# Attention scores on a graph: the linear weights, the square roots, the row order and the penalties moved between engines and stages

## The chip, the cores and the metric

One core of a Trainium2 chip runs the whole kernel in one launch. The metric is the device time of one execution in microseconds (us). TensorE is PE in the rows, VectorE is DVE, ScalarE is ACT, GpSimd is POOL and SyncE is SP.

## The reference

The kernel computes a graph attention layer and a mixture-of-experts layer on 2,500 nodes with 512 features; the change touches the first. Cut to what matters:

```python
x = x + gnn(layernorm(x), edge_index, W_e, W_r, a)      # 40,000 edges, sorted in the kernel by source
h_e = einsum('nf,hfd->hnd', xn, W_e)                    # 8 heads of 64
h_r = einsum('nf,hfd->hnd', xn, W_r)
a_src, a_dst, a_dif, a_abs, a_prd = split(a, 5, axis=1)
diff = h_r[:, dst] - h_r[:, src]
score = (h_e . a_src)[src] + (h_e . a_dst)[dst] + diff . a_dif + |diff| . a_abs + (h_r[src] * h_r[dst]) . a_prd
ex = exp(leaky_relu(score) - segment_max(...)[src]);  att = ex / segment_sum(ex)[src]
out = segment_sum(att * h_e[:, dst], src)
```

The terms of the score that are linear in h_e and h_r collapse to two vectors of 8 numbers a node: x times a matrix `lin` of 512 x 16 (8 columns for the source end, 8 for the other), where `lin` is W_e and W_r contracted with a_src, a_dst and a_dif.

## The kernel before, in words

`project_and_sort` is the first stage. Each engine has one list of instructions, in an order written out by hand, and semaphores between them.

- DVE sorts the 40,000 edge keys: `sort_inside(1)` to `sort_inside(9)` are n exchanges each, then `merge_near(m)` and `merge_inside()` for m = 1 to 5, then two merges (m = 6, 7) that need TensorE to turn the keys. Between them it makes the sums of the layer norm (`prepare(n, True)`), finishes the square roots (`prepare(n, False)`, for the blocks of `STAT_PARTS`: 0 to 3, 4 to 11, 12 to 19), makes `lin` (`weigh`), and finishes two blocks of table rows at a time (`finish(i)`: blocks 2i and 2i+1; it needs their squares and their linear terms `lin_sb`).
- PE counts edges into blocks (`count_blocks`, 20 small matmuls that follow ACT's `tally`), then goes through 20 blocks b: it turns block b+1 (`turn`), projects block b on W_r (`project_r`), takes its bf16 parts off (`take_mid`, `take_hi`), projects it on W_e (`project_e`) and makes the linear terms of block b-2 (`project_lin`). Five places in that order, numbered 2b (after `take_mid`) and 2b+1 (the end of block b), hold the turns of the sort keys: `KEY_TURNS`. PE waits there for `key_out`, and DVE's `come_back` waits for the turn.
- ACT makes the tallies, the square roots (`take_root(0)` among the tallies, `take_root(1)` ahead of the 20 blocks, `take_root(2)` in block 1), and for each block `normalise(b+2)`, `turned(b+1)` and the copies out of PSUM. `prepare(n, False)` on DVE waits for `take_root(n)` on ACT. `normalise(4)` and `normalise(12)` are the first that need the roots of parts 1 and 2.

`score_edges` is the second stage; it begins when every engine has ended the first. It takes 84 groups n of 512 edges. POOL gathers four tiles of rows a group (`RING` = 4 groups ahead), SP broadcasts the group's local row numbers (`spread`), DVE makes a one-hot of them, PE fetches the source rows with it (`fetch`), DVE subtracts, PE turns the difference, ACT takes |d| and a linear function of it, DVE multiplies, and PE reduces over the heads. Ahead of group 0 stand: the loads of `raw_a` and the write of `local_d` (SP, both ahead of the first `spread`), `heads`, `extra`, `cin`, `by_abs`, `by_square` (DVE, PE and ACT wait for them), and seven `penalties` (a matmul `pick` on PE and a pass on DVE each). Behind group 1 stands `lead_penalties`, one scan over 3,071 columns on DVE. `strip_scores` puts one further DVE instruction (512 columns) into each of four groups, once in 14 groups.

Of the kernel before, what the change touches and what calls it, by code (L numbers as in the profile page):

```python
# [9 lines left out]
ALU = mybir.AluOpType  # L10
# [33 lines left out]
SQUARED = frozenset(())  # L44
STAT_PARTS = (slice(0, 4), slice(4, 12), slice(12, NB))
KEY_TURNS = (29, 31, 34, 36, 38)
# [55 lines left out]
def project_and_sort(nc, k, sem, x, src, dst, we, wr, a, table_d, he_d):  # L102
# [8 lines left out]
    XB, SB, XT, AR = 6, 6, 4, 5  # L111
    with ExitStack() as ctx:
# [3 lines left out]
        a_all = s.sb("a_all", [P, HEADS, 4 * D])  # L116
        prod = s.sb("prod", [P, CH, HEADS, D])
        lin = s.sb("lin", [P, CH, 2 * HEADS])
        dif = s.sb("dif", [P, CH, HEADS])
# [34 lines left out]
        spare = prod[:, :, :, :].rearrange("p c h d -> p (c h d)")  # L154
# [10 lines left out]
        xin = [sem(f"x_in{c}") for c in range(5)]  # L165
        wrin, wein, ain = sem("w_r_in"), sem("w_e_in"), sem("a_in")
        lines_made, ident_made, number_made, window_made, made = sem("lines_made"), sem("ident_made"), sem("number_made"), sem("window_made"), sem("constants_made")
        stats, rready, rdone, normed = sem("stats"), sem("var_ready"), sem("root_done"), sem("norm_ready")
        linr, xn_ready, tp, xt_ready = sem("lin_ready"), sem("xn_ready"), sem("x_turned"), sem("xt_ready")
# [7 lines left out]
        key_out, key_turned = sem("key_out"), sem("key_turned")  # L177

        with nc.Block() as block:
            @block.sync  # L180
            def _(sp):
# [19 lines left out]
                for b in range(NB):  # L201
                    sp.wait_ge(he_ready, b + 1)
                    sp.dma_start(he_d[b * P:(b + 1) * P, :], he[:, b % 2, :]).then_inc(he_out[b % 2], 16)
                for j in range(2):
                    sp.wait_ge(he_out[j], 16 * NB // 2)

            @block.gpsimd
            def _(pool):
# [26 lines left out]
                                        fill=1.0, base=1, pattern=[[-1, P]], channel_multiplier=1))  # L235
                link(pool.memset(k["pick"][:, :, :, :, :], 0.0))
# [13 lines left out]
            def _(act):  # L250
                act.dma_start(a_all[:, :, 0:3 * D], a[:, 0:3 * D].partition_broadcast(P)).then_inc(ain, 16)
                act.dma_start(a_all[:, :, 3 * D:], a[:, 4 * D:].partition_broadcast(P)).then_inc(ain, 16)
# [56 lines left out]

                for t in range(8):  # L310
                    tally(t)
# [28 lines left out]
            def _(pe):  # L340
# [58 lines left out]

                pe.wait_ge(window_made, 1)  # L400
# [17 lines left out]
                project_lin(NB - 2)  # L418
                project_lin(NB - 1)
                pe.wait_ge(key_out, 6)  # L420
# [3 lines left out]
            def _(dve):  # L424
# [22 lines left out]
                def weigh():  # L447

                    dve.wait_ge(ain, 32)
                    dve.wait_ge(wrin, 16 * CH)  # L450
                    dve.wait_ge(wein, 16 * CH)
                    w4e = w_e[:, :, :].rearrange("p c (h d) -> p c h d", h=HEADS)
                    w4r = w_r[:, :, :].rearrange("p c (h d) -> p c h d", h=HEADS)
                    for w, piece, out in ((w4r, 2, dif[:, :, :]), (w4e, 0, lin[:, :, 0:HEADS]), (w4e, 1, lin[:, :, HEADS:])):
                        link(dve.tensor_tensor(prod[:, :, :, :], w, bcast(a_all[:, :, piece * D:(piece + 1) * D], 1, CH), ALU.mult))
                        link(dve.tensor_reduce(out, prod[:, :, :, :], AX_X, ALU.add))
                    mark(dve.tensor_tensor(lin[:, :, 0:HEADS], lin[:, :, 0:HEADS], dif[:, :, :], ALU.subtract))
                    dve.tensor_tensor(lin[:, :, HEADS:], lin[:, :, HEADS:], dif[:, :, :], ALU.add).then_inc(linr, 1)
                    link(dve.tensor_scalar(a_all[:, :, 3 * D:], a_all[:, :, 3 * D:], 0.5, None, ALU.mult))

                def finish(i):
# [4 lines left out]
                    link(dve.tensor_tensor(both, both, bcast(a_all[:, :, 3 * D:], 1, 2), ALU.mult))  # L466
# [98 lines left out]
                weigh()  # L565
# [3 lines left out]
                prepare(2, True)  # L569
                sort_inside(7)  # L570
                prepare(2, False)
                sort_inside(8)
                finish(0)
                sort_inside(9)
                insert_pads()
                for m in range(1, 6):
                    merge_near(m)
                    merge_inside()
                    finish(m)
                for m in (6, 7):  # L580
# [6 lines left out]
                    if m == 6:  # L587
                        finish(6)

                dve.nop().then_inc(key_out, 1)  # L590
                finish(7)
# [15 lines left out]
                link(dve.scalar_tensor_tensor(k["local_rows"][:, :], is_pad, float(P), part, ALU.mult, ALU.add))  # L607
                link(dve.tensor_scalar(part, whole, 12, None, ALU.logical_shift_right))
# [3 lines left out]
                finish(8)  # L612
                finish(9)
# [9 lines left out]
def score_edges(nc, k, sem, a, table_d, local_d):  # L623
# [6 lines left out]
    RING = 4  # L630
    hrs, lins, att = k["hrs"], k["lins"], k["att"]
    with ExitStack() as ctx:
# [5 lines left out]
        raw = s.sb("raw_a", [P, 2, CH])  # L638
# [3 lines left out]
        heads = s.sb("heads", [P, 62])  # L642
        by_abs = s.sb("by_abs", [P, CH, 62])
        by_square = s.sb("by_square", [P, CH, 62])
# [11 lines left out]
        cin = s.sb("cin", [1, 2, CH, 16, 2])  # L656
# [6 lines left out]
        ain, wready = sem("score_a_in"), sem("score_weights")  # L663
        picked, penned = sem("runs_picked"), sem("penalties")
        got = [sem(f"rows_in{j}") for j in range(RING)]
        local_out, locs = sem("locals_out"), [sem(f"locals_in{j}") for j in range(RING)]
# [8 lines left out]
        multiplied = lambda n: CH * sum(i not in SQUARED for i in range(n + 1))  # L675

        with nc.Block() as block:  # L677
            @block.sync
            def _(sp):
                for half in range(2):  # L680
                    for n, piece in enumerate((3, 4)):
                        sp.dma_start(raw[half * D:(half + 1) * D, n, :],
                                     a.rearrange("(c t) f -> f c t", t=2)[piece * D:(piece + 1) * D, :, half],
                                     allow_slow_non_contiguous=True).then_inc(ain, 16)
                sp.dma_start(local_d[:, :], k["local_rows"][0:G, :]).then_inc(local_out, 16)
                sp.wait_ge(local_out, 16)
# [21 lines left out]
            def _(dve):  # L708
                link = k["dve_chain"].on(dve)
                mark = k["dve_chain"].mark  # L710
                mark(dve.memset(heads[:, :], 0.0))
                mark(dve.memset(extra[:, :, :, :, :, :], 0.0))
                link(dve.memset(cin[:, :, :, :, :], 0.0))
                mark(dve.memset(heads[0:D, 30:31], 1.0))
                mark(dve.memset(heads[D:P, 31:32], 1.0))
                dve.wait_ge(ain, 64)
                link(dve.tensor_scalar(raw[:, 1, :], raw[:, 1, :], -0.5, None, ALU.mult))
# [958 lines left out]
```

## Time and profile before

| | us |
|---|---|
| median of 3 runs | 1646.72 (1646.37 to 1648.43) |
| the profiled execution | 1648.01 |
| its span, first to last instruction | 1646.3 |
| first stage | 0 to 234.4 |
| second stage, first group's first subtraction | 247.74 |

The span is 1.7 us shorter than the execution that it was taken from, and that execution 1.3 us longer than the median. Times in rows are from the start of the span.

### The profile page before, as it was taken

What the parts mean: (1) busy time and instruction counts of PE and PEld (TensorE: products, weight loads), DVE (VectorE), ACT (ScalarE), POOL (GpSimd) and SP (SyncE); (2) the same over time, 40 slices, a digit from 0 to 9 for tenths busy, and PEclk for the clock granted to TensorE, in tenths of its full rate; (3) what the DMA queues carried; (4) which work ended last, traced back from release to release, by engine and by line L of the source; (5) the groups of instructions that cost most, each with busy time, mean ns of one, the idle gap of its engine ahead of it and who ended that gap; (6) DMA issues with size and microseconds to landing.
All of it is one profiled execution on the core that took longest, in us unless ns stands there. A gap on an engine that the chain in (4) does not pass through costs nothing. (4 is left out here: it accounts for less than half of the span.)

```text
span 1646.3 us, 25232 instructions
## 1 busy us (share of the span) xinstructions
PE 1305.9 (79%) x6421; PEld 745.9 (45%) x6422; DVE 1212.5 (74%) x2399; ACT 980.8 (60%) x2411; POOL 884.1 (54%) x982
## 2 busy tenths in 40 slices
PE   5799948999999999995688888888880702999950
PEld 1355524555555555552344444444440301777730
DVE  8898578999999999997588888888889320222216
ACT  3455516998989898984677777777770300333310
POOL 2000036666666666662677777777767055555520
PEclk9899968999999999997799999999995955999985
DMA  6111136777777777760877766676660821333329
GB/s 209 39 58 53 58 113 172 213 205 199 208 198 207 199 207 199 208 184 2 288 194 209 200 198 201 200 201 199 199 187 2 306 103 33 115 127 127 128 96 348
DMA packets 114111, 271.34 MB, mean 165 GB/s; under 512 B 27650, under 2 KB 43766, under 8 KB 113738
## 3 DMA queue, kind: packets, MB, share of 16 engines
q0 software_dynamic: 64160, 207.60, 43.4%
q1 hardware_dynamic: 47754, 61.26, 11.1%
q10 hardware_dynamic: 2080, 1.05, 0.2%
q8 instruction: 58, 0.95, 0.2%
q14 instruction: 59, 0.48, 0.1%
HBM read 236.42 MB, written 33.43 MB: 164 GB/s over the span
## 5 line engine op out<-in xcount | busy, mean ns | idle before, releaser
L1096 PE MATMUL m_ps<-msg,hot 128*128 128x512 f32 x672 | 368.4, 638 | 73.8 <-ACT msg L1038 64.6
L701 POOL DMA_INDIRECT x_sb<-table_d,target x336 | 333.0, 991 | 174.6 <-PE d_ps L871 86.8
L1015 POOL DMA_INDIRECT g<-he_d,target x336 | 339.6, 1011 | 132.9 <-issue 78.7
L945 ACT ACTIVATE uv<-ab,raw_a 128x512 f32<-128x512 f32 x336 | 274.3, 816 | 11.3
L858 PE MATMUL gs_ps<-room,hot_t 128*128 x1008 | 276.4, 384 | 1.7 <-DVE hot_t L724 1.7
L1059 DVE TENSOR_TENSOR msg<-g,room 128x384 f32<-128x384 f32 x336 | 185.7, 553 | 84.9 <-DMA g<-he_d,target 81.4
L731 DVE TENSOR_TENSOR x_sb<-x_sb,gs_ps 128x512 f32<-128x512 f32 x336 | 229.2, 682 | 17.8 <-PE lin_ps L862 11.5
L940 ACT ACTIVATE ab<-d_ps 128x512 f32<-128x512 f32 x336 | 196.1, 584 | 73.4 <-PE d_ps L871 71.5
L1038 ACT ACTIVATE msg<-g,room 128x64 f32<-128x64 f32 x672 | 170.2, 339 | 111.9 <-DMA g<-he_d,target 111.7
L735 DVE TENSOR_TENSOR uv<-uv,ab 128x512 f32<-128x512 f32 x336 | 230.2, 685 | 3.3 <-ACT uv L945 2.8
L1066 DVE TENSOR_TENSOR room<-m_ps,room 128x512 f32 x336 | 229.8, 684 | 0.6
L871 PE MATMUL d_ps<-ident,x_sb 128*128 128x128 f32 x1344 | 213.9, 282 | 6.9 <-DVE x_sb L731 6.1
L1098 PEld LDWEIGHTS den_ps<-room,hot 128*128 128x128 f32 x672 | 128.7, 191 | 162.6 <-issue 162.6
L871 PEld LDWEIGHTS d_ps<-ident,x_sb 128*128 128x128 f32 x1344 | 141.8, 141 | 51.4 <-DVE x_sb L731 12.8
L858 PEld LDWEIGHTS gs_ps<-room,hot_t 128*128 128x128 bf16 x1008 | 92.6, 98 | 111.7 <-issue 69.8
L1096 PEld LDWEIGHTS m_ps<-msg,hot 128*128 128x128 f32 x672 | 102.5, 193 | 78.7 <-issue 77.9
L1532 DVE TENSOR_TENSOR hid_in<-h_ps,b_sb 128x256 f32<-128x256 f32 x47 | 20.0, 425 | 145.1 <-PE h_ps L1468 145.1
L245 POOL DMA_DIRECT2D table_d<-row x20 | 11.1, 562 | 204.9 <-DVE row L471 204.9
L1030 ACT ACTIVATE off<-iota,local 128x128 f32<-128x128 f32 x336 | 107.0, 395 | 0.3 <-PEq L677 0.3
L891 PE MATMUL sc_ps<-uv,heads 128*32 128x512 f32 x672 | 91.2, 615 | 12.0 <-DVE uv L735 12.0
L1098 PE MATMUL den_ps<-room,hot 128*128 128x8 f32 x672 | 96.0, 215 | 0.0
L1468 PE MATMUL h_ps<-w_sb,xt 128*128 x376 | 90.6, 385 | 0.0
(284 smaller groups left out, 1711.7 us busy)
## 6 DMA issues: line engine op xcount, KB each, us to landing
x_sb<-local_d SPq DMA_DIRECT2D x84, 128.0 KB
w_sb<-in_L_ffn_W_dram SPq DMA_DIRECT2D x16, 512.0 KB, 9.2
pair_rows<-pairs_d SPq DMA_DIRECT2D x8, 1024.0 KB, 13.0
x_sb<-table_d,target POOLq DMA_INDIRECT x336
g<-he_d,target POOLq DMA_INDIRECT x336
table_d<-row POOLq DMA_DIRECT2D x20, 260.0 KB, 2.6
he_d<-he SPq DMA_DIRECT2D x20, 256.0 KB, 2.0
xn_d<-xn SPq DMA_DIRECT2D x10, 512.0 KB, 4.0
```

The lines of the kernel that those rows point to most:

```text
L701: pool.indirect_dma_start(gd[:, r, t, :], None, table_d, bass.IndirectOffsetOnAxis(ap=k["target"][:, q + t:q + t + 1], axis=0)).then_inc(g ...
L731: dve.tensor_tensor(row, row, gs_ps[:, (GT * n + t) % 3, :], ALU.subtract).then_inc(dready, 1)
L735: dve.tensor_tensor(uv[:, n % 2, c, :], uv[:, n % 2, c, :], ab[:, n % 2, c, :], ALU.mult).then_inc(vr, 1)
L858: pe.matmul(gs_ps[:, (GT * n + t) % 3, :], h, hrs[:, bass.ds(blk, 1), piece, :].rearrange("p a f -> p (a f)"), start=(piece == 0), stop=(p ...
L871: last = pe.transpose(d_ps[:, c % 2, t * P:(t + 1) * P], gd[:, n % RING, t, c * P:(c + 1) * P], k["ident"][:, :])
L940: act.activation(ab[:, j, c, :], d_ps[:, c % 2, :], ACT.Abs).then_inc(abr, 1)
L945: act.activation(uv[:, j, c, :], ab[:, j, c, :], ACT.Identity, bias=raw[:, 0, c:c + 1], scale=raw[:, 1, c:c + 1]).then_inc(ur, 1)
L1015: pool.indirect_dma_start(g[:, r, t, :, :, :].rearrange("p c h d -> p (c h d)"), None, he_d, bass.IndirectOffsetOnAxis(ap=k["target"][:, q ...
L1059: dve.tensor_tensor(msg[:, r, t, 0:HV, :, :], g[:, r, t, 0:HV, :, :], bcast(weight, 3, D), ALU.mult).then_inc(made, 1)
L1066: dve.tensor_tensor(to, m_ps[:, i % BK, :], to, ALU.add).then_inc(added, 1)
L1096: pe.matmul(m_ps[:, i % BK, :], hot[:, r, t, :], msg[:, r, t, :, :, :].rearrange("p c h d -> p (c h d)"), start=True, stop=True).then_inc( ...
L1098: pe.matmul(den_ps[:, bass.ds(blocks[t] * HEADS, HEADS)], hot[:, r, t, :], att[:, tg * GT + t, :, strip, :], start=False, stop=True, skip_ ...
```

## The change

- `lin` is made on PE: ACT's DMA queue loads three pieces of `a` turned (`a_rows`, six loads of single elements), POOL lays them on diagonals (`a_cols`), PE turns W_r and W_e in eight steps of four transposes (`turn_weights`: four ahead of `turn(0)`, four behind the last count), ACT copies each out (`keep_turned_weights`), and PE multiplies: 32 matmuls with 16 columns (`weigh`), ahead of block 0. DVE's `weigh` goes.
- `take_root(1)` moves from ahead of the blocks to block 1, `take_root(2)` from block 1 to block 7. On DVE, `prepare(2, False)` moves behind `sort_inside(8)`.
- `finish(0)` comes ahead of `sort_inside(8)`, `finish(1)` behind `prepare(2, False)`, and each later one a merge sooner; `finish(9)` ahead of the last `key_out`. `KEY_TURNS` are later.
- `raw_a` is loaded by ACT's queue at the kernel's start (four loads of single elements, ahead of ACT's first instruction), and `heads`, `cin` and its scaling are POOL's, in the first stage. `local_d` is written by SP at the end of the first stage.
- In the second stage the seven penalties go to groups 2 to 8 (`PICK_AT` = 2), and the scan becomes six of 512 columns in groups 9 to 14 (`LEAD_AT` = 9). The unused branch `SQUARED` goes, with `by_abs` and `by_square`.

```diff
-KEY_TURNS = (29, 31, 34, 36, 38)
+KEY_TURNS = (33, 34, 38, 40, 41)
...
-    XB, SB, XT, AR = 6, 6, 4, 5
+    XB, SB, XT, AR = 6, 6, 4, 4
...
+                sp.wait_ge(key_out, 6)
+                sp.dma_start(local_d[:, :], k["local_rows"][0:G, :]).then_inc(local_out, 16)
...
@@ scalar
-                act.dma_start(a_all[:, :, 0:3 * D], a[:, 0:3 * D].partition_broadcast(P)).then_inc(ain, 16)
-                act.dma_start(a_all[:, :, 3 * D:], a[:, 4 * D:].partition_broadcast(P)).then_inc(ain, 16)
+                for half in range(2):
+                    for piece in range(3):
+                        act.dma_start(a_rows[half * D:(half + 1) * D, piece, :],
+                                      a.rearrange("(c t) f -> f c t", t=2)[piece * D:(piece + 1) * D, :, half],
+                                      allow_slow_non_contiguous=True).then_inc(arin, 16)
+                act.dma_start(a_prd[:, :, :], a[:, 4 * D:].partition_broadcast(P)).then_inc(ain, 16)
+                for half in range(2):
+                    for n, piece in enumerate((3, 4)):
+                        act.dma_start(k["raw_a"][half * D:(half + 1) * D, n, :],
+                                      a.rearrange("(c t) f -> f c t", t=2)[piece * D:(piece + 1) * D, :, half],
+                                      allow_slow_non_contiguous=True).then_inc(rawin, 16)
...
+                for i in range(4):
+                    keep_turned_weights(i)
                 turned(0)
                 for t in range(14, NB):
                     tally(t)
-                take_root(1)
+                for i in range(4, 8):
+                    keep_turned_weights(i)
+                act.wait_ge(lin_summed, 1)
+                act.copy(lin[:, :, :], l_ps[:, 0:CH * 2 * HEADS].rearrange("p (c x) -> p c x", c=CH)).then_inc(linr, 1)
                 for b in range(NB):
                     if b == 1:
+                        take_root(1)
+                    if b == 7:
                         take_root(2)
...
@@ tensor
+                def weigh():
+                    pe.wait_ge(cols_ready, 1)
+                    pe.wait_ge(w_kept, 2 * CH)
+                    for c in range(CH):
+                        for i in range(2 * CH):
+                            last = pe.matmul(l_ps[:, c * 2 * HEADS:(c + 1) * 2 * HEADS], w_t[:, i // CH, i % CH, c * P:(c + 1) * P],
+                                             a_cols[:, 1 - i // CH, i % CH, :], start=(i == 0), stop=(i == 2 * CH - 1))
+                    last.then_inc(lin_summed, 1)
...
                 pe.wait_ge(ident_made, 2)
+                for i in range(4):
+                    turn_weights(i)
                 turn(0)
                 count_blocks(14, NB)
+                for i in range(4, 8):
+                    turn_weights(i)
+                weigh()
...
@@ vector
-                weigh()
                 prepare(1, True)
                 sort_inside(6)
                 prepare(1, False)
                 prepare(2, True)
+                dve.wait_ge(ain, 16)
+                link(dve.tensor_scalar(a_prd[:, :, :], a_prd[:, :, :], 0.5, None, ALU.mult))
                 sort_inside(7)
+                finish(0)
+                sort_inside(8)
                 prepare(2, False)
-                sort_inside(8)
-                finish(0)
+                finish(1)
                 sort_inside(9)
...
@@ score_edges, tensor
                 for n in range(G + 2):
                     if n < G:
                         blocks = blocks_of(n)
+                    if 0 <= n - PICK_AT <= TG:
+                        pick(n - PICK_AT)
```

## Rows read from the trace of the kernel before

**Rows 1.** The timeline of DVE: start, length, line, tiles.

```profile
25.93 2.29 DVE L455 TENSOR_TENSOR prod<-w_r,a_all 128x2048 f32<-128x2048 f32 x1
...
40.53 4.85 DVE L436 BATCH_NORM_STATS2 st<-x_sb 128x6 f32<-128x512 f32 x8
...
63.31 0.20 DVE L94 RECIPROCAL rstd<-root 128x8 f32<-128x8 f32 x1
...
64.48 0.42 DVE L483 TENSOR_TENSOR key<-key 128x256 f32<-128x256 f32 x1
...
70.84 1.23 DVE L466 TENSOR_TENSOR sq<-sq,a_all 128x1024 f32<-128x1024 f32 x1
...
78.58 0.18 DVE L470 TENSOR_TENSOR lin_src<-lin_sb,own 128x16 f32<-128x16 f32 x1 [5.26 <-ACT lin_sb L308]
...
229.52 0.32 DVE L620 TENSOR_TENSOR lins<-lin_rest,lins 128x160 bf16<-128x160 f32 x1
```

**Rows 2.** Groups of DVE, 0 to 300 us: busy, mean, idle before, releaser.

```profile
L517 DVE COPY key<-k_ps 128x512 f32<-128x512 f32 x4 | 2.8, 692 | 16.2 <-PE k_ps L397 16.2
...
L470 DVE TENSOR_TENSOR lin_src<-lin_sb,own 128x16 f32<-128x16 f32 x10 | 1.8, 175 | 9.7 <-ACT lin_sb L308 9.5
```

**Rows 3.** The timeline of PE in the first stage.

```profile
50.45 4.97 PE L356 MATMUL r_ps<-w_r,xt 128*128 128x512 f32 x8
...
69.54 0.64 PE L346 MATMUL t_ps<-ident,xn 128*128 128x128 f32 x4
...
77.31 0.96 PE L373 MATMUL l_ps<-lin,xt 128*128 128x16 f32 x8
78.12 0.64 PE L346 MATMUL t_ps<-ident,xn 128*128 128x128 f32 x4
```

**Rows 4.** The timeline of ACT at the start.

```profile
1.93 1.28 ACT L254 ACT_TABLE_LOAD   x1 [1.93 <-issue]
...
7.96 4.94 ACT L261 ACTIVATE above<-src_i,block_edge 80x500 bf16<-80x500 int32 x8 [4.54 <-DMA dst_i<-in_dst_dram]
```

**Rows 5.** The timelines of POOL and SP where the stages meet.

```profile
228.56 1.07 POOL L245 DMA_DIRECT2D table_d<-row  x2 [1.73 <-DVE row L471]
...
244.03 0.94 POOL L701 DMA_INDIRECT x_sb<-table_d,target  x1 [0.30 <-issue]
...
234.39 2.69 SPq L682 DMA_DIRECT2D raw_a<-in_L_gnn_a_dram  x4
...
240.69 45.38 SPq L690 DMA_DIRECT2D x_sb<-local_d  x11
```

**Rows 6.** PE's timeline, then PE and clock by stretch (columns in the header).

```profile
1278.27 4.34 PE L1265 MATMUL t_ps<-ident,xn 128*128 128x128 f32 x20 [39.76 <-DVE xn L1292]
...
core 0: us, PE busy (x) PEld busy (x) DVE busy (x) ACT busy (x) POOL busy (x), PEclk, DMA share, GB/s
...
1282.00:1286.00 4.00, 3.87 (x13) 1.01 (x12) 2.60 (x6) 1.13 (x2) 0.00 (x0) 1.00 1.02 378
...
216.45:220.45 4.00, 2.89 (x25) 2.73 (x24) 3.72 (x10) 1.99 (x5) 0.13 (x1) 1.00 0.52 199
220.45:222.00 1.55, 0.43 (x3) 0.32 (x2) 1.40 (x3) 0.17 (x1) 0.00 (x0) 0.50 0.00 0
```

**Rows 7.** DVE's timeline: first subtractions of groups 1 and 5.

```profile
252.47 0.68 DVE L731 TENSOR_TENSOR x_sb<-x_sb,gs_ps 128x512 f32<-128x512 f32 x1
...
283.57 0.68 DVE L731 TENSOR_TENSOR x_sb<-x_sb,gs_ps 128x512 f32<-128x512 f32 x1
```

**Rows 8.** DVE's timeline, one row a group: groups 17 to 20.

```profile
357.50 0.25 DVE L741 TENSOR_REDUCE lin_sum<-lin_ps 128x32 f32<-128x96 f32 x1
...
363.19 0.25 DVE L741 TENSOR_REDUCE lin_sum<-lin_ps 128x32 f32<-128x96 f32 x1
...
369.45 0.25 DVE L741 TENSOR_REDUCE lin_sum<-lin_ps 128x32 f32<-128x96 f32 x1
...
376.29 0.24 DVE L741 TENSOR_REDUCE lin_sum<-lin_ps 128x32 f32<-128x96 f32 x1
```

More of the change, by code:

```diff
@@ L163, in project_and_sort @@
         k_ps = s.ps("k_ps", [P, F])
-        xin = [sem(f"x_in{c}") for c in range(5)]
+        xin, arin = [sem(f"x_in{c}") for c in range(5)], sem("a_rows_in")
         wrin, wein, ain = sem("w_r_in"), sem("w_e_in"), sem("a_in")
@@ L235, in _ @@
                                         fill=1.0, base=1, pattern=[[-1, P]], channel_multiplier=1))
+                link(pool.memset(a_cols[:, :, :, :], 0.0))
+                pool.wait_ge(arin, 16 * 6)
+                diagonal = lambda w, half, first: a_cols[half * D:(half + 1) * D, w, :, :].rearrange("p c x -> p (c x)")[:, first + half::2 * HEADS + 2]
+                for half in range(2):
+                    part = slice(half * D, (half + 1) * D)
+                    link(pool.tensor_copy(diagonal(0, half, 0), a_rows[part, 0, :]))
+                    link(pool.tensor_copy(diagonal(0, half, HEADS), a_rows[part, 1, :]))
+                    link(pool.tensor_scalar(diagonal(1, half, 0), a_rows[part, 2, :], -1.0, None, ALU.mult))
+                    link(pool.tensor_copy(diagonal(1, half, HEADS), a_rows[part, 2, :]))
+                pool.nop().then_inc(cols_ready, 1)
+                link(pool.memset(k["heads"][:, :], 0.0))
+                link(pool.memset(k["heads"][0:D, 30:31], 1.0))
+                link(pool.memset(k["heads"][D:P, 31:32], 1.0))
+                link(pool.memset(k["cin"][:, :, :, :, :], 0.0))
+                pool.wait_ge(rawin, 64)
+                link(pool.tensor_scalar(k["raw_a"][:, 1, :], k["raw_a"][:, 1, :], -0.5, None, ALU.mult))
                 link(pool.memset(k["pick"][:, :, :, :, :], 0.0))
@@ L578, in _ @@
                     merge_inside()
-                    finish(m)
+                    finish(m + 1)
                 for m in (6, 7):
@@ L630, in score_edges @@
     RING = 4
+    PICK_AT, LEAD_AT = 2, 2 + TG + 1
     hrs, lins, att = k["hrs"], k["lins"], k["att"]
+    raw, heads, cin = k["raw_a"], k["heads"], k["cin"]
     with ExitStack() as ctx:
@@ L661, in score_edges @@
         lin_row = lin_ps[:, 0, :]
-        ain, wready = sem("score_a_in"), sem("score_weights")
-        picked, penned = sem("runs_picked"), sem("penalties")
+        picked = sem("runs_picked")
         got = [sem(f"rows_in{j}") for j in range(RING)]
-        local_out, locs = sem("locals_out"), [sem(f"locals_in{j}") for j in range(RING)]
+        locs = [sem(f"locals_in{j}") for j in range(RING)]
         lin_summed = sem("lin_summed")
@@ L674, in score_edges @@
         order = [(tg, st) for tg in range(TG) for st in range(STRIPS)]
-        multiplied = lambda n: CH * sum(i not in SQUARED for i in range(n + 1))
+        use = lambda n, t: GT * n + t + min(max(n - PICK_AT + 1, 0), TG + 1)
         with nc.Block() as block:
@@ L679, in _ @@
             def _(sp):
[L680 to L686, printed above, removed]
                 for n, (tg, st) in enumerate(order):
@@ L774, in strip_scores @@
                         link(dve.tensor_reduce(fpart[:, tg:tg + 1], first, AX_X, ALU.max))
-                penalties()
+                link(dve.memset(extra[:, :, :, :, :, :], 0.0))
                 one_hot(0)
-                multiplies = lambda n: 0 <= n < G and n not in SQUARED
+                inside = lambda n: 0 <= n < G
                 for n in range(G + 2):
+                    if 0 <= n - PICK_AT <= TG:
+                        penalties(n - PICK_AT)
                     if n < G:
                         subtract(n, 0)
-                    if multiplies(n - 2):
+                    if inside(n - 2):
                         times(n - 2, 3)
@@ L879, in reduce @@
                     column = slice(30 - 2 * st, 62 - 2 * st)
[L880 to L892 removed]
+                    pe.wait_ge(vr, CH * n + CH)
+                    for c in range(CH):
+                        last = pe.matmul(sc_ps[32 * c:32 * (c + 1), :], heads[:, column], uv[:, n % 2, c, :],
+                                         start=(st == 0), stop=False, tile_position=(0, 32 * c), skip_group_check=True)
                     last.then_inc(red, 1)
@@ L1629, in kernel_body @@
                     runs=e.sb("runs", [P, F], BF16),
+                    raw_a=e.sb("raw_a", [P, 2, CH]), heads=e.sb("heads", [P, 62]),
+                    cin=e.sb("cin", [1, 2, CH, 16, 2]),
                 )
-                project_and_sort(nc, k, sem, x, src, dst, we, wr, a, table_d, he_d)
+                project_and_sort(nc, k, sem, x, src, dst, we, wr, a, table_d, he_d, local_d)
                 score_edges(nc, k, sem, a, table_d, local_d)
```

152 lines of the change are left out of this document (65 added, 87 removed).

## Prediction

> **What bounds the kernel now.** The page first (PE 79% of the span, DVE 74%), but an average over stages decides nothing; then the timelines of DVE, PE and ACT over the first stage. DVE has work from 8 us to its last instruction there, which ends at 229.84 [rows 1], and sat idle only where it asked PE or ACT for something: 16.2 us for the turned keys and 9.7 us for linear terms [rows 2]. PE goes through the blocks at one per 8.58 us (69.54 to 78.12) with no gap [rows 3]. So the first stage has two long streams side by side, hand-tied at a few places, and what matters is which of them waits at each tie. Then the timelines where the stages meet: table rows leave at 228.56, the second stage starts at 234.4 [rows 5], and its first subtraction comes 13.3 us later. In its groups PE is full, and a group takes 5.69 us (357.50 to 363.19) [rows 8].
>
> **DVE's weigh.** Removed: 25.93 to 40.53, 14.6 us of DVE [rows 1]. That is worth 14.6 us only if nothing that DVE waits for stays where it is.
>
> **When PE begins block 0 (T0).** ACT now issues eleven loads ahead of its first instruction. SP issued four such loads of single elements in 2.69 us, 0.67 each [rows 5]; ten of them, 0.6 for the broadcast and the start at 0.8 give 8.1; table load and first root 1.5 [rows 4]; first tally at 9.7 instead of 7.96. (It also frees DVE and ACT from the long broadcast ahead of `dst`, worth nothing, since ACT is the later one.) A tally takes 0.62 (4.94 for 8) [rows 4]: fourteen and a root 8.7, so 18.4, and PE's count ends 0.6 behind, at 19.0. Four steps of transposes follow. At the low clock level 20 transposes took 4.34 us [rows 6], so a step is 0.87: 22.5; `turn(0)` 23.4; ACT's copy 24.1; six tallies 27.8, PE's last count 28.4; four more steps 31.9, and the last copy 32.6. `AR` 5 to 4 costs nothing: PE follows each tally within one. The POOL work for `a_cols` (eight small instructions from about 9) and the weights' loads are in by then (DVE read both weights from 25.93 on without a wait [rows 1]).
>
> Then PE's `weigh`: 32 fp32 matmuls, two instructions each, 64, of just the form of `project_lin`, of which 8 take 0.81 us (77.31 to 78.12) [rows 3]. At the full level 6.5 us; at the low one twice that, 13. Here the level is the open price. PE is low when this begins. Twenty transposes back to back brought it up: 0.50 before (PE had idled 39.8 us), 1.00 from 1282 on [rows 6]. On the other side, a stretch of mostly `project_lin` matmuls, 2.89 of 4.00 us busy, ended with the level down to 0.50 at 220.45 [rows 6]; back to back they may do better. Between 6.5 and 13 I take 8.4: a low start, then the full level. T0 = 32.6 + 8.4 = 41.0; bounds 39.1 and 45.6, and in the latter case block 0 starts low too: its first projection took 4.97 in place of about 3.6 us [rows 3], so 47.2.
>
> The Trainium skill ("TensorE: Matmul & The Clock Gate", Part 4: PE-mode transpose) says that transposes do not count as work for the clock. By that rule PE's `weigh` would be low throughout and the sum that of rival A; the trace disagrees, with its 20 transposes.
>
> **The square roots: the wait that takes weigh's place.** `take_root(1)` now stands on ACT behind all of block 0, which follows T0: about T0 + 8.7 = 49.7. DVE arrives for it at 36 (25.93 and 5.6 for the sums and 4.8 for six exchanges). It waits some 13 us: weigh's whole saving. Next `finish(0)` asks for block 1's linear terms (block 3 of PE, T0 + 32.8): 9 us, in place of 5.26 before [rows 1]. Then the long one: `take_root(2)` stands behind ACT's `keep_mid(6)`. PE's blocks 0 and 1 take 7.8 (no linear part), blocks 2 to 5 8.58 each, and block 6 up to `take_hi` 7.8, with copy and root 1.3: T0 + 58.9 = 99.9. DVE, with `sort_inside(8)` done, is there at about 80 and waits 20 us. Queued behind it are `finish(1)`, the rest of the sort, and all else of the stage.
>
> From there DVE has: its stream from 63.31 to 229.84 of before, 166.5, less its waits 25.9 [rows 2], less `sort_inside(8)` (64.48 to 70.84, 6.4) and `finish(0)` (70.84 to 78.58 less 5.26, and 0.3: 2.8), now done earlier [rows 1]: 131.5. Its ties to PE, at the new `KEY_TURNS`: the first, second and fourth turns find PE already waiting (0.7 each for the turn itself, and PE stands still for them); place 38 is reached at T0 + 168.6, DVE is there at T0 + 162.6: 6.0. So DVE ends at T0 + 58.9 + 131.5 + 8.1 = T0 + 198.5 = 239.5, against 229.84. The moved `finish` calls are the same ten and cost nothing by place (rows 2 ahead of the ring's reuse: block 10 needs `finish(2)`'s rows out at about T0 + 90, which they are). PE has spare time at the end, so its 11 to 20 us of new work cost only through T0.
>
> **The meeting of the stages.** Before, the last rows (issued 228.56 + 1.07, landing 2.6 later as the page has it) were out near 231.7, and the stage began 2.7 later [rows 5]. After: `local_d` leaves at the last `key_out`, 2.2 ahead of DVE's end, and its write takes 3.6 (237.1 to 240.69) [rows 5]: DVE's end + 1.4, + 2.7. Second stage at 239.5 + 4.1 = 243.6, before 234.4: **+9.2**.
>
> **Its prologue.** Gone: 2.69 of `raw_a` issues, the write, the memsets and penalties ahead of group 0. Next late are the gathers: group 1's last was issued at 244.03, 9.6 into the stage [rows 5], and lands about 3 later, so group 1's first subtraction comes at 13.2 into it, not 18.1 (252.47) [rows 7]: **-4.9**. PE has group 0's tiles fetched by then; the clock is low in both.
>
> **Scan and penalties.** Before, groups 1 to 5 took 31.1 us (252.47 to 283.57) [rows 7] where four at 5.69 are 22.8: the scan, and PE's fall to the low level behind it, cost 8.3. After: one more DVE instruction of 512 columns in a group made it 6.26 (0.57 more), the two later ones 0.48; one with a scan 6.84 (1.15) [rows 8]. Six penalties at 0.5, a short one at 0.15, six scans at about 1.07 (the form before ran a little shorter per column) and the ends 0.2: 9.8. PE's `pick`, a fifth of a microsecond, is under DVE's. **+1.5**; from -8.3 (all hidden) to +2.2. The heads', cin's and raw_a's work on POOL is free: POOL idles there until `finish(0)`. `SQUARED` was empty: nothing.
>
> **Sum.** +9.2 - 4.9 + 1.5 = +5.8. On the profiled execution (1648.01, span 1646.3) 1653.8; on the median 1646.72, which is what is forecast, **1652.5**. A measurement tells about 0.2%, 3.3 us, from no change.
>
> **Rivals.**
> A, PE's `weigh` wholly at the low level: T0 acts as 47.2, +6.2: 1658.7. For it: `project_lin` did not hold the level at 220; against it: the transposes ahead. By the skill's rule this is the case.
> B, ACT's loads back up, SP's own had to queue in the first 20 us, and the first tally comes 3 us later: 1655.5. For it: 2,560 single elements; against: SP's four went at an even 0.67.
> C, faster: the second stage's pieces hide in DVE's free time. Place: groups 2 to 14; price: the 9.8 in the loop falls to about 0, so 5.8 - 9.8 = -4.0: 1642.7. It decides only once they cost under 0.7 together. DVE has 0.2 free per group, against it stand the 0.48 to 1.15 of [rows 8].
> D, the waits move but cost little: T0 at its floor (every step of PE at the full level, 36.5 to 37.5), and the loop at +0: -4 and -1.5 against the forecast, no change: 1647. For it: PE worked on and off since 9 us.
>
> **How the numbers follow.** Forecast 0.48, with its own range 1649.5 to 1655.5 (T0 39 to 43, loop +0 to +2.2); A 0.25; B 0.07; C 0.08; D 0.12. Range 1645.5 to 1660: it leaves out C and a tail of A and B. Faster by over 0.2%: C and a little of D, 0.10. Within 0.2% (to 1650.0): most of D and the forecast's low end, 0.17. Slower: 0.73.
>
> **What would show it.** In the trace after: T0 (the second `turn`, block 1's) near 41, with `weigh`'s 64 matmuls at 0.1 or 0.2 each; DVE idle for `root` twice, about 13 and 20 us, the second ending near 100; DVE's last instruction near 239.5; first subtraction of group 1 13.2 into the second stage; groups 3 to 8 at 6.2 and 10 to 14 at 6.8. It is wrong if ACT reaches block 7 before 85, if the root waits are short, or if groups 2 to 14 keep 5.7.

## The result, and the profile after

The changed kernel ran at a median of 1660.63 us (1658.14 to 1662.18, four runs) beside 1646.55 of the kernel before: 1.0082 times its time (1.0064 to 1.0099), 14 us more. The sign was forecast, the size was not: +5.8 had been worked out, and +14.1 lies just above the range. The profiled execution, read below, is the fastest of the four (1658.14, span 1656.4, 10.1 longer than before's span).

ACT's timeline after: start, length, line.

```profile
0.80 4.91 ACTq L274 DMA_DIRECT2D a_rows<-in_L_gnn_a_dram  x6
5.75 0.77 ACTq L277 DMA_DIRECT2D a_prd<-in_L_gnn_a_dram  x1
6.54 4.58 ACTq L280 DMA_DIRECT2D raw_a<-in_L_gnn_a_dram  x4
11.16 1.28 ACT L284 ACT_TABLE_LOAD   x1 [11.16 <-issue]
...
12.56 3.71 ACT L291 ACTIVATE above<-src_i,block_edge 80x500 bf16<-80x500 int32 x6
...
59.24 0.22 ACT L295 ACTIVATE root<-var 128x8 f32<-128x8 f32 x1
...
109.64 0.22 ACT L295 ACTIVATE root<-var 128x8 f32<-128x8 f32 x1
```

The first six loads of single elements take 0.82 each and the last four 1.15, not 0.67, so the first tally starts at 12.56, 2.9 later than forecast (7.96 before [rows 4]). Both roots stand nearly 10 us later than forecast (59.24 for 49.7, 109.64 for 99.9).

PE's timeline after, and the granted clock of that stretch (second fence: us, PE busy, PEld busy, DVE, ACT, POOL, PEclk, DMA share, GB/s).

```profile
30.75 1.97 PE L448 MATMUL r_ps<-ident,w_e 128*128 128x128 f32 x8
32.51 1.91 PE L448 MATMUL e_ps<-ident,w_e 128*128 128x128 f32 x8
35.19 13.81 PE L457 MATMUL l_ps<-a_cols,w_turned 128*128 128x16 f32 x64 [0.77 <-ACT w_turned L342]
48.84 1.09 PE L387 MATMUL t_ps<-ident,xn 128*128 128x128 f32 x4
49.72 5.09 PE L397 MATMUL r_ps<-w_r,xt 128*128 128x512 f32 x8
...
74.58 0.64 PE L387 MATMUL t_ps<-ident,xn 128*128 128x128 f32 x4
```

```profile
35.20:37.00 1.80, 1.80 (x9) 1.80 (x9) 1.33 (x4) 0.00 (x0) 0.00 (x0) 0.50 0.00 0
37.00:49.00 12.00, 12.00 (x58) 12.00 (x58) 0.00 (x0) 0.00 (x0) 0.00 (x0) 0.50 0.01 1
```

PE's `weigh` stays at the 1.2 GHz level (0.50) from end to end, though PE is never idle in it: 13.81 us for 64. T0 is 48.84. PEld is as busy as PE: each of the 64 has 128 columns of weights to load for 16 of work. The last row is block 4's turn, from where PE goes on at 8.58 a block: it is 5.0 later than before (69.54 [rows 3]).

DVE's waits in the first stage (us in total, times, longest), and its last instruction there.

```profile
DVE rstd L93 <- ACT root L295: 46.3, 3, 23.0
DVE key L571 <- PE k_ps L438: 8.8, 4, 6.0
DVE lin_src L524 <- ACT lin_sb L338: 8.8, 1, 8.8
```

```profile
250.05 0.33 DVE L675 TENSOR_TENSOR lins<-lin_rest,lins 128x160 bf16<-128x160 f32 x1
```

The waits for turned keys and linear terms, 25.9 us before [rows 2], are 17.6; in their place, and in that of the 14.6 us of DVE's `weigh` [rows 1], stand 46.3 us for roots. DVE ends at 250.38, 20.5 later than before.

Where the stages meet, on SP; then on DVE the first subtraction of group 1, and `lin_sum` of groups 7, 8, 10, 11, 14 and 18.

```profile
248.15 0.33 SPq L207 DMA_DIRECT2D local_d<-local_rows  x1
252.92 1.74 SPq L734 DMA_DIRECT2D x_sb<-local_d  x4
```

```profile
267.23 1.28 DVE L764 TENSOR_TENSOR x_sb<-x_sb,gs_ps 128x512 f32<-128x512 f32 x2 [2.66 <-DMA x_sb<-table_d,target]
...
307.75 0.24 DVE L774 TENSOR_REDUCE lin_sum<-lin_ps 128x32 f32<-128x96 f32 x1
...
313.42 0.24 DVE L774 TENSOR_REDUCE lin_sum<-lin_ps 128x32 f32<-128x96 f32 x1
...
325.73 0.24 DVE L774 TENSOR_REDUCE lin_sum<-lin_ps 128x32 f32<-128x96 f32 x1
...
332.56 0.24 DVE L774 TENSOR_REDUCE lin_sum<-lin_ps 128x32 f32<-128x96 f32 x1
...
353.09 0.24 DVE L774 TENSOR_REDUCE lin_sum<-lin_ps 128x32 f32<-128x96 f32 x1
...
377.52 0.25 DVE L774 TENSOR_REDUCE lin_sum<-lin_ps 128x32 f32<-128x96 f32 x1
```

The second stage starts at 252.9 (18.5 later [rows 5]); a group with a scan takes 6.83. At group 18 the kernel is 14.3 behind (377.52 against 363.19 [rows 8]), and 14.2 at the last group. Behind that, in stages that the change leaves as they were, this execution made up 4.5 us (PE's first turn of the expert layer at 1287.99 against 1278.27 [rows 6]). So the 14.3 of this trace and the 14.1 of the medians agree better than the two profiled spans do, which is in part chance.

### The profile page after: what moved, and what is told of

Same layout as the page of the kernel before. It is cut to its first block and busy times, and to the rows that moved or that the text cites. A ratio compares the mean times of both kernels' runs of the same rounds, so it can differ in the third digit from the quotient of the medians.

```text
span 1656.4 us, 25442 instructions
## 1 busy us (share of the span) xinstructions
PE 1324.8 (80%) x6517; PEld 766.4 (46%) x6518; DVE 1196.3 (72%) x2389; ACT 984.5 (59%) x2420; POOL 885.1 (53%) x996
## 5 line engine op out<-in xcount | busy, mean ns | idle before, releaser
L764 DVE TENSOR_TENSOR x_sb<-x_sb,gs_ps 128x512 f32<-128x512 f32 x336 | 228.1, 680 | 17.9 <-DMA x_sb<-table_d,target 7.7
```

Source lines behind the costliest of these rows:

```text
L764: dve.tensor_tensor(row, row, gs_ps[:, use(n, t) % 3, :], ALU.subtract).then_inc(dready, 1)
```

## The experiments

The twelve runs (ten kernels, two of them run twice) came in three sets, each beside the kernel before. In the second set (1804.3 behind the difference) before took 1804.3 us. The first stage took no longer there (DVE's end at 212.35 and 212.05 for one kernel in two sets), so across sets both the ratios and the differences in us are to be looked at. "Block 4's turn" is when PE starts it, "from there" the time to the end of DVE's last instruction in the first stage, "DVE's end".

| kernel | weigh on | block 4's turn | from there | DVE's end | ratio to before (95%) | us against before |
|---|---|---|---|---|---|---|
| before | DVE | 69.54 | 160.3 | 229.84 | 1 | 0 |
| after | PE | 74.58 | 175.8 | 250.38 | 1.0082 (1.0064 to 1.0099) | +14.1 |
| x1_roots | PE | 74.30 | 174.0 | 248.31 | 1.0072 (1.0058 to 1.0085) | +12.6 |
| x2_roots_keys | PE | 72.81 | 165.9 | 238.72 | 1.0026 (1.0015 to 1.0036) | +3.3 |
| x3_raw_sp | PE | 65.44 | 175.4 | 240.86 | 1.0054 (1.0041 to 1.0068) | +8.2 |
| x4_second_stage | DVE | 69.37 | 160.3 | 229.64 | 0.9986 (0.9977 to 0.9995) | -2.6 |
| x5_first_stage | PE | 70.84 | 175.6 | 246.41 | 1.0097 (1.0077 to 1.0116) | +19.4 (1804.3) |
| x6_swapped | PE | 66.51 | 175.6 | 242.08 | 1.0040 (1.0028 to 1.0053) | +8.9 (1804.3) |
| x7_order | DVE | 52.71 | 159.6 | 212.35 | 0.9908 (0.9888 to 0.9928) | -15.2 (1804.3) |
| x8_order_second | DVE | 52.90 | 159.7 | 212.55 | 0.9853 (0.9830 to 0.9876) | -25.2 (1804.3) |
| y1_pe_repaired | PE | 61.73 | 154.7 | 216.41 | 0.9893 (0.9878 to 0.9909) | -17.0 |
| y2_weigh_later | DVE | 72.56 | 160.3 | 232.87 | 1.0013 (1.0004 to 1.0022) | +3.0 |
| y3_both_again | DVE | 53.32 | 157.9 | 211.19 | 0.9863 (0.9848 to 0.9878) | -21.6 |
| y4_order_again | DVE | 52.76 | 159.3 | 212.05 | 0.9887 (0.9872 to 0.9902) | -16.5 |

### The roots alone: x1_roots

```diff
                 for i in range(4, 8):
                     keep_turned_weights(i)
+                take_root(1)
                 act.wait_ge(lin_summed, 1)
...
-                    if b == 1:
-                        take_root(1)
-                    if b == 7:
+                    if b == 1:
                         take_root(2)
```

> The kernel after, with only two instructions of ACT moved: take_root(1) ahead of the wait for PE's weigh, take_root(2) into block 1; nothing is left out. The forecast's theory (the root waits set DVE's end): the trace of after has DVE idle 46.3 us for roots, 23.0 in the longest wait; with them gone DVE ends 15 to 20 us sooner, and the kernel runs 15 us below after. Stream theory (PE's pass over the 20 blocks, which starts at T0 and stands still only for key turns placed late, sets when DVE can end; a root wait only moves the idle time forward): the waits come back as waits for turned keys, DVE's end moves from 250.4 to about 249, the kernel runs 1 us below after.

The same order of PE with 46 us less of root waits: DVE's end moved by 2.1, the median by 1.9, to 1658.76. DVE's waits in the first stage:

```profile
DVE lin_src L523 <- ACT lin_sb L338: 28.3, 5, 17.1
DVE key L570 <- PE k_ps L437: 15.7, 4, 8.0
...
DVE sq L519 <- ACT room L319: 13.6, 1, 13.6
...
DVE rstd L93 <- ACT root L295: 3.1, 1, 3.1
```

The 46.3 us for roots are 3.1, and the other waits rose from 17.6 to 57.6: the idle time moved behind the work that used to follow it. The forecast had priced the root waits as the place where the time is lost; they were where it shows. The stream theory holds in both of its times (249 and 1 us); that the waits would come back as waits for turned keys was half of it, since most came back as waits for linear terms (28.3) and for ACT's step ahead of them in `finish` (13.6).

### The roots and the key turns: x2_roots_keys

```diff
-KEY_TURNS = (33, 34, 38, 40, 41)
+KEY_TURNS = (31, 33, 36, 37, 39)
```

> As the run with both roots early, and KEY_TURNS (31, 33, 36, 37, 39) in place of (33, 34, 38, 40, 41); nothing is left out. The forecast's theory: the places of the turns cost only their 6 us wait of the fourth one, so at most 6 us below the run with the roots alone. Stream theory: with DVE early the places are what holds it; DVE ends near 240.5, 9 us below the run with the roots alone and 10 below after. Neither reaches the kernel before: T0 itself is 20 us later than in before.

DVE's end 238.72, 9.6 below the roots alone, and the median 9.2 lower (1649.52). Of the 9.6, 1.5 came ahead of block 4, where PE's `weigh` took 11.82 in place of 13.81 (its first 2 us at the full level), and 8.1 behind it. The places of the turns in PE's order are the next tie. They can probably be this early only because DVE is there in time; the turns without the roots were not run.

### The loads: x3_raw_sp

```diff
@@ sync
+                for half in range(2):
+                    for n, piece in enumerate((3, 4)):
+                        sp.dma_start(k["raw_a"][half * D:(half + 1) * D, n, :], ...).then_inc(rawin, 16)
@@ scalar
-                for half in range(2):
-                    for n, piece in enumerate((3, 4)):
-                        act.dma_start(k["raw_a"][half * D:(half + 1) * D, n, :], ...).then_inc(rawin, 16)
```

> The kernel after, with raw_a's four loads of single elements on SP behind the loads of x in place of ACT's first list; nothing is left out. Theory of the loads (in after they took 6.54 to 11.12 on ACT, ahead of its first table load, and everything behind them follows: tallies, T0, PE's blocks, DVE's end): first tally at about 8, T0 and DVE's end 4.5 us sooner, kernel 4.5 us below after. Rival (T0 is not what sets the first stage's end, or PE waits for the weights or a_cols instead): the first tally is 4.5 sooner and the kernel within 1.5 us of after.

ACT's and PE's timelines, and the granted clock:

```profile
7.42 4.91 ACT L291 ACTIVATE above<-src_i,block_edge 80x500 bf16<-80x500 int32 x8
...
100.49 0.22 ACT L295 ACTIVATE root<-var 128x8 f32<-128x8 f32 x1
```

```profile
29.54 10.94 PE L457 MATMUL l_ps<-a_cols,w_turned 128*128 128x16 f32 x64 [0.77 <-ACT w_turned L342]
40.32 1.09 PE L387 MATMUL t_ps<-ident,xn 128*128 128x128 f32 x4
```

```profile
28.00:28.50 0.50, 0.50 (x4) 0.37 (x2) 0.47 (x8) 0.50 (x1) 0.00 (x0) 0.50 1.03 385
31.50:32.50 1.00, 1.00 (x11) 1.00 (x10) 0.97 (x4) 0.00 (x0) 0.00 (x0) 1.00 0.11 17
33.50:40.40 6.90, 6.90 (x34) 6.90 (x35) 0.03 (x1) 0.00 (x0) 5.30 (x8) 0.50 0.00 0
```

The first tally came 5.1 us sooner, T0 8.5 (weigh itself was 2.9 shorter, its first 3 us at the full level), the second root 9.2, DVE's end 9.5, the median 6.3. At the last group of the second stage the 9.2 are still there (754.35 for 763.59); behind it some of this is lost again, and no run says to what. T0, root and end move as one; from block 4's turn on it is 175.4 us, as in after (175.8). By chance this kernel is a test of the forecast's arithmetic: it has the T0 that was forecast (40.32 for 41.0), and the second root at 100.5 for 99.9 and DVE's end at 240.9 for 239.5 follow. Up to the end of the first stage, what was wrong was T0, for the most part.

### PE's weigh turned round: x6_swapped

```diff
-                    for c in range(CH):
-                        for i in range(2 * CH):
-                            last = pe.matmul(l_ps[:, c * 2 * HEADS:(c + 1) * 2 * HEADS], w_t[:, i // CH, i % CH, c * P:(c + 1) * P],
-                                             a_cols[:, 1 - i // CH, i % CH, :], start=(i == 0), stop=(i == 2 * CH - 1))
+                    for i in range(2 * CH):
+                        last = pe.matmul(l_ps[0:2 * HEADS, :], a_cols[:, 1 - i // CH, i % CH, :], w_t[:, i // CH, i % CH, :],
+                                         start=(i == 0), stop=(i == 2 * CH - 1))
+                    ... (ACT copies the 16 x 512 out, four transposes bring it back)
```

> The kernel after with PE's weigh turned round: a_cols is the stationary side and 8 matmuls of 512 columns go over the turned weights, then ACT copies 16 x 512 and 4 transposes bring it back; nothing is left out. It asks for the clock level of this stretch. In after the 64 instructions of 16 columns took 13.81 us, low throughout. Block 0's projection in after (8 instructions of 512 columns) took 5.09 with a low start against 3.60 at the full level, so the long ones raise the level within a few us. Theory (the narrow matmuls keep the level down): 16 instructions of 512 columns take about 9 us, 2 more for the copy and transposes, T0 near 46 and the kernel 2 to 4 below after. Rival (the level is down because of what PE did before, whatever comes now): 14.4 us and 2, T0 near 52, the kernel 2 to 3 above after.

PE's timeline, and the granted clock:

```profile
34.61 7.03 PE L460 MATMUL l_ps<-w_turned,a_cols 128*16 128x512 f32 x16 [0.77 <-ACT w_turned L344]
42.30 0.42 PE L465 MATMUL l_ps<-ident,he 16*128 16x16 f32 x4 [0.67 <-ACT he L361]
```

```profile
34.60:41.60 7.00, 6.99 (x16) 1.46 (x16) 1.59 (x5) 0.00 (x0) 0.00 (x0) 1.00 0.00 0
```

Sixteen instructions of 512 columns ran at 2.4 GHz, 7.03 us in place of 13.81; the next turn came at 42.65, 6.2 sooner than in after, and DVE's end at 242.08, 8.3 sooner (block 0 starts at the full level as well); from block 4's turn on it is again 175.6. Both theories had priced this too high: I had expected 9 us or 14. The comparison with after is not quite a fair one, since here the level had risen just ahead (the last eight transposes took 1.65 in place of 1.91). The next kernel is fairer: there the narrow ones begin at the full level too.

### The halves apart: x4_second_stage and x5_first_stage

The first is `project_and_sort` of before and `score_edges` of after; the second is the reverse.

> The kernel before with only the second stage's part of the change: raw_a loaded in the first stage (by SP, behind x), heads, cin and raw_a's scaling on POOL, local_d written at the end of the first stage, penalties in groups 2 to 8, the scan in groups 9 to 14; nothing is left out. By what the trace of after showed (prologue 4.4 shorter, loop +0.2, end to stage start 2.5 against 4.6): 4 to 6 us below before. By the forecast's terms (-4.9, +1.5, 0.5 at the meeting): 4 us below. Rival (the write of local_d was hidden behind the table rows, and low-clock stretches of PE eat the rest): within 1.5 us of before.

> The kernel after with the second stage of before (raw_a loaded again there, local_d written there, penalties ahead of group 0, the scan behind group 1); nothing of the reference is left out. If the two halves of the change add up (the second stage's part alone gave 2.6 us): 2 to 4 us above after, about 17 above before, all of it in the first stage, which ends near 250.4 on DVE. By the forecast's terms the first stage would be worth 9.2: 1655.5. Rival (the first stage of after costs less than its 20 us because something else is hidden there): under 12 above before.

The second stage's part alone is worth 0.14% (2.6 us at the median, 0.8 to 3.8 by its interval; the two profiled spans differ by 5.1), between both expectations and too near them to choose. The first stage's part alone is 0.97%, or 19.4 us (13.9 to 20.9 by its interval). With the second's it gives 0.83% for the whole, where 0.82% was measured, or 16.8 us, where 14.1 were: they add up within these intervals. By the forecast's terms the first stage should have cost 0.6%, 9 to 10 us, and under 12 was the rival's. The expectation missed one thing: DVE's end was 246.41 and not near 250.4, since in this execution the level was up ahead of `weigh` and for its first microsecond, and T0 came at 45.69.

In x5_first_stage the clock was at the full level when weigh began:

```profile
30.43 1.09 PE L445 MATMUL r_ps<-ident,w_e 128*128 128x128 f32 x8
31.36 1.04 PE L445 MATMUL e_ps<-ident,w_e 128*128 128x128 f32 x8
33.32 12.53 PE L454 MATMUL l_ps<-a_cols,w_turned 128*128 128x16 f32 x64 [0.93 <-ACT w_turned L339]
```

```profile
33.30:34.30 1.00, 0.98 (x9) 1.00 (x10) 0.97 (x3) 0.00 (x0) 0.00 (x0) 1.00 0.00 0
34.30:35.30 1.00, 1.00 (x9) 1.00 (x8) 0.97 (x4) 0.00 (x0) 0.00 (x0) 0.71 0.00 0
35.30:45.70 10.40, 10.40 (x51) 10.40 (x50) 2.52 (x7) 0.00 (x0) 0.00 (x0) 0.50 0.01 2
```

The transposes still ran at it (eight in 1.09, in place of 1.97), it fell within 2 us of the start of the narrow matmuls, and it stayed down for the other ten, PE busy throughout. In x3_raw_sp the level was up for their first 3 us and then fell, with nothing but such matmuls on PE since 29.54, back to back. So it is the shape, and no idle time, that costs some 6 us here. Which side of the shape, the 16 columns or the weight load that each of the 64 has, no run separates. At the full level x3_raw_sp did 11 of the narrow ones in a microsecond, so 64 would be about 6 us (an estimate from that row): turning them round saves no work on PE, it keeps the level.

### Another order, weigh on DVE: x7_order and y4_order_again

Before had lost its time to order too: PE stood 14.1 us in block 0, whose end waits on ACT for a buffer, and ACT stood behind `take_root(1)`, which needs sums that DVE makes behind its own `weigh`. PE's timeline and ACT's, before:

```profile
49.20 0.61 PE L378 MATMUL r_ps<-room,minus_bf 128*128 128x512 bf16 x1 [14.05 <-ACT room L289]
```

```profile
46.30 0.21 ACT L265 ACTIVATE root<-var 128x8 f32<-128x8 f32 x1 [20.86 <-DVE var L441]
```


```diff
-KEY_TURNS = (29, 31, 34, 36, 38)
+KEY_TURNS = (29, 30, 33, 34, 36)
...
-                    if b == 1:
+                    if b == 5:
                         take_root(2)
...
                 sort_inside(5)
-                weigh()
                 prepare(1, True)
                 sort_inside(6)
                 prepare(1, False)
-                prepare(2, True)
+                weigh()
                 sort_inside(7)
-                prepare(2, False)
+                prepare(2, True)
                 sort_inside(8)
                 finish(0)
                 sort_inside(9)
+                prepare(2, False)
```

> The kernel before with only its order changed: DVE's weigh moved behind prepare(1, False), take_root(2) to block 5, prepare(2, True) behind sort_inside(7), prepare(2, False) behind sort_inside(9), KEY_TURNS (29, 30, 33, 34, 36); nothing is left out. It asks whether the goal of the change (DVE's 25.9 us of idle time in the first stage) can be had with weigh on DVE. Stream theory: block 1 starts when lin and the first roots are there, the PE stream is then early enough for every key turn, DVE ends near 210 in place of 229.8 and the kernel runs 20 us below before. Rival (ring of rows, writes of h_e or the copies on ACT hold PE, the same 25.9 us of waits appear elsewhere): DVE's end within 5 us of 229.8 and the kernel within 5 us of before.

> The new order of the first stage alone, once more beside the other runs of this set; nothing is left out. As measured before: DVE's end 17.5 us below before's, ratio 0.989 to 0.991, 15 to 18 us below before.

DVE's end 212.35 and 212.05 (210 expected), ratios 0.9908 and 0.9887, that is 15.2 and 16.5 us below before where 20 had been expected. DVE's waits in the first stage, y4_order_again:

```profile
DVE key L517 <- PE k_ps L397: 6.2, 4, 2.3
...
DVE lin_src L470 <- ACT lin_sb L308: 1.7, 2, 1.1
```

The 25.9 us [rows 2] are 7.9, with all of `weigh`'s 14.6 us still on DVE. PE's block 4 starts at 52.8 in place of 69.54, and the time from there is that of before (159.3).

### Weigh's place alone: y2_weigh_later

```diff
                 sort_inside(5)
-                weigh()
                 prepare(1, True)
                 sort_inside(6)
                 prepare(1, False)
+                weigh()
```

> The kernel before with one edit: DVE's weigh behind prepare(1, False); nothing is left out. Stream theory: PE no longer stands 14 us for room in block 0 (which follows the roots of part 1), but 18 us for lin in block 2, and the key turns stay at (29, 31, 34, 36, 38): DVE ends at 231, the kernel within 3 us of before. Rival (what the whole new order won, all came from weigh's place): 15 us or more below before.

DVE's end 232.87, +3.0 us. PE's stall moved one block on and grew (17.9 us in place of 14.1): block 4 starts 3.0 later, and DVE's end is 3.0 later. The size is the expected one, the reason isn't: I had PE waiting for `lin` in block 2, but it waits at the end of block 1, again for ACT, which stands behind `take_root(2)`:

```profile
57.94 0.21 ACT L265 ACTIVATE root<-var 128x8 f32<-128x8 f32 x1 [21.67 <-DVE var L441]
```

So the second root had to move with it. What the root, the places of `prepare(2, ...)` and the key turns are worth one by one in this order was not run.

### Both: x8_order_second, y3_both_again; and PE's version repaired: y1_pe_repaired

The first two are one kernel, x7_order's edit with x4_second_stage's. The third is after with x1, x3 and x6, the row order of before, and `KEY_TURNS = (27, 29, 32, 34, 36)`.

> The kernel with the new order of the first stage and the second stage's part of the change together; nothing is left out. If they add up: 22 to 23 us below before (20 and the 2.6 measured for the second part alone). Rival (both live off the same idle time at the meeting of the stages): no further gain over the new order alone.

> The kernel with the new order of the first stage and the second stage's part of the change once more, beside the other runs of this set; nothing is left out. As measured before: ratio to before 0.985 to 0.988, that is 20 to 25 us.

> The kernel after with all that its traces showed late taken back, and weigh still on PE: operands swapped (that stretch took 7.03 us at the full level), raw_a's loads on SP, both roots early, finish and prepare(2, False) in the order of before, KEY_TURNS (27, 29, 32, 34, 36); nothing is left out. Stream theory: T0 near 37, no wait for a late tie, DVE ends at 217 to 221 in place of 229.8, and with the second stage's 2.6 the kernel runs 10 to 14 us below before. Rival (with weigh on PE the first blocks are too late for any order of the rest): DVE ends at 230 or later and the kernel is not below before by more than 3 us.

The new order with the second stage's part runs at 1625.61 (1624.22 to 1626.78), 21.6 below before and 35 below after; in the second set it is 25.2 below before. Over the order alone the second part is worth 5.2 in this set and 10.0 in the second, and alone it was 2.6. So it doesn't vanish beside the order, as the rival had it, but its size is not settled. PE's version repaired runs at 1630.20, DVE's end 216.41 (217 to 221 expected), T0 37.86, 3 us better than the hoped-for 10 to 14. So weigh may stand on PE, and it beats before there. It stays 5 us behind the order with `weigh` on DVE at DVE's end: from block 4 on it is 3.2 shorter without weigh on DVE, but block 4 starts 8.4 later, behind PE's eight steps and its sum.

## Why the prediction was right in sign and wrong in size

By its own steps, with what each should have been; they add up to 14.3.

| step | forecast | measured |
|---|---|---|
| first tally | 9.7 | 12.56 |
| PE's `weigh` | 8.4 | 13.65 to the next turn |
| T0 | 41.0 | 48.84 |
| second root | T0 + 58.9 | T0 + 60.8 |
| from there to DVE's end | 139.6 | 140.7 |
| DVE's end | 239.5 | 250.38 |
| to the second stage | +4.1 | +2.5 |
| second stage starts later by | 9.2 | 18.5 |
| prologue, to group 1's first subtraction | -4.9 | -3.8 |
| scan and penalties, from there to group 18 | +1.5 | -0.4 |
| sum | +5.8 | +14.3 (+14.1 at the median) |

**The step that failed is T0**, by 7.8 us, where +14.3 is 8.5 above +5.8, in two terms (the steps between them took 0.3 less than forecast). The larger, 5.3, is the level of PE's `weigh`: 8.4 was taken between 6.5 and 13 because 20 transposes had once raised the clock [rows 6]. The row on the other side, the fall during `project_lin`'s matmuls [rows 6], was the nearer one: the same form of instruction, and x3_raw_sp and x5_first_stage show it happen from the full level. Rival A had this with its price (+6.2) and was given 0.25. On the rule of the Trainium skill ("TensorE: Matmul & The Clock Gate", Part 4: PE-mode transpose) that transposes do not count as work for the clock: it led to the right time by way of a reason that these runs don't bear out. In x5_first_stage it was the matmuls of 16 columns that lost the full level, behind transposes that had it, and in x3_raw_sp the level rose from 0.50 behind sixteen transposes (25.10 to 28.78), to 1.00 as `weigh` began. The smaller term, 2.9, is the price of a load of single elements: 0.67 was taken from SP's four at 234.4; ACT's cost 0.82 and 1.15, and the same four on SP in x3_raw_sp, at 21.7 us, 1.38 (5.52 in all). So it isn't a matter of ACT's queue alone; what sets it was not tried. That was rival B (+3, 0.07). The two rivals don't exclude one another, and the forecast had no case in which both came true: +6.2, +3 and +5.8 make +15.0, or 1661.7. Each was held against the forecast singly, and the range ended at 1660, below their sum.

The second root's 1.9 beyond T0 is block 0 on a low start (9.46 to the next turn in place of 7.8), which rival A had in its 47.2.

**Right:** that weigh's 14.6 us on DVE would not be gained since both roots hang on PE's blocks; from T0 to DVE's end the chain was right within 3 us (201.5 for 198.5), with waits of 23.0 and 19.7 for 13 and 20 (7.8 of the first one's excess is T0). "Rows 2 ahead of the ring's reuse" was not quite so: ACT waited 2.4 us once for a table row to leave, with no trace of it at DVE's end. A group with a scan took 6.83 for 6.84, a group with a penalty 6.11 for 6.2. The smaller terms were off by 1 to 2 us and made up for one another: the meeting by 1.6 and the scan and penalties by 1.9 too high, the prologue by 1.1 too low. Rival C (the pieces hide) fell: a group with a piece takes 6.11 or 6.83, not 5.69.

**Where the loss was, which the forecast didn't say.** It spoke of root waits as the loss, and x1_roots took them away for 2 us. The table splits the 20.5 us at DVE's end in another way. PE's blocks run 5.0 later (74.58 for 69.54), and from block 4 on it takes 175.8 in place of 160.3: 15.5 more. That second number is 175.4 to 175.8 in each of the four kernels with after's whole order, whatever happened ahead of block 4, and in two sets, and 160.3 in each of the three with before's key turns, so it belongs to the order. x1 and x2 bring it to 165.9 by roots and key turns together; y1, which also takes the row order back and has still earlier key turns, to 154.7; what the row order does alone was not run. Even in x3_raw_sp, whose PE is 4.1 ahead of before's at block 4, DVE ends 11.0 later.

## What to carry to other kernels

Work taken off one engine of two hand-tied streams can be worth nothing until the ties are moved with it, as here: look for when the other engine's long stream really starts to run and put every tie where both arrive together. Here that alone was worth 16.5 us without moving any work, while moving 14.6 us of work, with a late start of PE's blocks and the ties set later, cost 1%, and moved with its ties put right (y1_pe_repaired) it still ended the stage 5 us later than the new order that left it on DVE. A look at when a fixed mark of the slower stream passes, and at the time from it to the end, tells a late stream from a bad order. When two rivals don't exclude one another, forecast the case in which both hold. Where many matmuls of few columns stand in a row, as the 64 of PE's `weigh`, try them turned round, so that the wide side streams.

## What the runs showed of the hardware

- Under matmuls of 16 columns with a new weight load each, TensorE's granted clock fell from 1.00 to 0.50 (within 2 us of their start in x5_first_stage, after 3 us in x3_raw_sp) and stayed there for 10 and for 7, at 100% busy; sixteen of 512 columns in the same place held 1.00. At 0.50 the first cost 0.216 us each, 13.81 in all; at 1.00 the second cost 0.44, 7.03 in all.
- The granted clock rose from 0.50 to 1.00 behind nothing but transposes of 128 x 128 fp32, 20 before [rows 6] and 16 in x3_raw_sp.
- A load of 64 x 4 single elements issued from ACT took 0.82 us of its queue for the first six and 1.15 for the last four; from SP 1.38 at 21.7 us (x3_raw_sp) and 0.67 at 234.4 [rows 5].
- The same kernel took 1630.8 us in one set of runs and 1789.1 in another. The two profiles differ most behind the first two stages; PE's busy time and the granted clock from 800 to 1000 us:

y4_order_again:

```profile
800.00:1000.00 200.00, 169.46 (x606) 94.44 (x606) 165.68 (x306) 151.44 (x612) 153.67 (x153) 1.00 0.71 201
```

x7_order:

```profile
800.00:1000.00 200.00, 142.26 (x437) 78.26 (x437) 122.02 (x218) 118.76 (x460) 116.80 (x118) 0.79 0.60 179
```

PE did 437 instructions there in place of 606, at 0.79. Whether the clock is the cause or follows from PE's idle time was not tried, nor what differs between the two sets.
